# A graph network on one core: where the output bias of the last convolution is added

## The reference

```python
def _sage_conv(x, edge_index, W_l, b, W_r):
    agg = segment_sum(x[src], dst, num_segments=x.shape[0])
    mean = agg / clip(cnt, 1.0)[:, None]
    return mean @ W_l + b + x @ W_r

h = relu(_sage_conv(h, edge_index, W1_l, b1, W1_r))   # 64 -> 128
x = x + _sage_conv(h, edge_index, W2_l, b2, W2_r)     # 128 -> 64
```

## Time and profile before

| | us |
|---|---|
| median of 3 runs | 7730.98 |
| lowest and highest | 7723.53, 7738.78 |
| the profiled execution | 7742.53 |
| its span from the first to the last instruction | 7740.3 |

### The profile page before, as it was taken

How to read it: one execution, slowest core, us unless ns; L and a number is a source line. 1 busy time by engine, 2 the same in 40 slices (tenths; PEclk the granted TensorE clock), 3 DMA queues, 4 the chain that set the end, 5 groups by cost and what they waited for, 6 DMA issues and landing times.

```text
span 7740.3 us, 169629 instructions
## 1 busy us (share of the span) xinstructions
PE 6713.2 (87%) x36506; PEld 3466.6 (45%) x36667; DVE 5131.9 (66%) x16509; ACT 3383.0 (44%) x5811; POOL 4929.5 (64%) x5691
## 2 busy tenths in 40 slices
PE   6999999975777767777759999999999899998998
PEld 4777777742333333333324444444444344443443
DVE  7888888865777777777746777777777733332322
ACT  5999999943545454545423333333333301110000
POOL 4333333327777777777757777777777466663777
PEclk9999999985556666666569999999999999998999
DMA  4333333342222222222222222222222266665765
GB/s 124 96 96 97 96 97 96 96 157 67 86 81 86 81 86 82 86 82 82 86 54 61 60 62 62 61 60 60 61 61 61 52 184 171 168 166 158 199 195 159
DMA packets 773996, 769.58 MB, mean 99 GB/s; under 512 B 242490, under 2 KB 585591, under 8 KB 773815
## 3 DMA queue, kind: packets, MB, share of 16 engines
q1 hardware_dynamic: 575703, 589.32, 24.5%
q0 software_dynamic: 147776, 160.99, 10.5%
q10 hardware_dynamic: 50400, 17.87, 1.0%
HBM read 581.15 MB, written 187.29 MB: 99 GB/s over the span
## 4 chain that ended last, share of the span: by engine, by line
PE 56%; POOL 13%; issue 12%; DVE 10%; DMA 4%; DVEq 2%; ACT 2%; another core or an unknown queue 0%; ACTq 0%; POOLq 0%; SPq 0%
POOL zone L1032 10%; PE ps L2549 8%; PE ps L2388 7%; PE ps L2187 6%; PE ps L2205 5%; PE ps L2212 4%; PE ps L2554 4%; PE ps L2380 3%; DMA zone<-tab_msg,idx 3%; POOL zone L1072 3%; DVE zone L1376 2%; PE ps L2352 2%; PE ps L2203 2%; PE ps L2407 2%; PE ps L2373 1%
## 5 line engine op out<-in xcount | busy, mean ns | idle before, releaser
L1032 POOL DMA_INDIRECT zone<-tab_msg,idx x1664 | 1729.2, 1039 | 526.6 <-issue 467.8
L1032 POOL DMA_INDIRECT zone<-tab_u,idx x1664 | 1580.0, 950 | 603.7 <-issue 479.6
L2026 ACT ACTIVATE zone<-ps 128x792 fp8e4<-128x792 f32 x1200 | 963.2, 830 | 990.8 <-PE ps L2352 973.5
L1376 DVE TENSOR_TENSOR zone<-ps,zone 128x512 f32<-128x512 f32 x1664 | 1063.1, 685 | 367.7 <-PE ps L2380 233.0
L2187 PE MATMUL ps<-zone 128*128 128x64 f32 (+1 forms) x6656 | 860.0, 287 | 341.3 <-DMA zone<-tab_msg,idx 337.3
L2352 PE MATMUL ps<-zone 128*128 128x396 bf16 x2400 | 898.5, 484 | 247.8 <-ACT zone L2026 147.7
L2187 PEld LDWEIGHTS ps<-zone 128*128 128x128 f32 (+1 forms) x6656 | 758.6, 198 | 492.8 <-issue 447.0
L2388 PE MATMUL ps<-zone,w_bas 128*64 128x512 f32 x3328 | 898.7, 618 | 0.0
L2549 PE MATMUL ps<-zone 128*128 128x512 fp8e4 x3332 | 842.6, 382 | 25.4 <-DMA zone<-adj 14.8
L1661 DVE TENSOR_SCALAR zone<-tT,zone 128x392 bf16<-128x392 f16 x2400 | 777.2, 324 | 0.0
L2052 ACT ACTIVATE zone<-ps 64x512 f32<-64x512 f32 x832 | 492.4, 592 | 491.1 <-PE ps L2373 479.6
(11 more groups left out here) (324 smaller groups left out, 10390.6 us busy)
## 6 DMA issues: line engine op xcount, KB each, us to landing
zone<-adj SPq DMA_DIRECT2D x238, 768.0 KB
adj<-zone SPq DMA_DIRECT2D x150, 784.0 KB
zone<-in_dst_row SPq DMA_DIRECT2D x832, 128.0 KB, 2.7
zone<-in_ea_T SPq DMA_DIRECT2D x416, 128.0 KB, 2.5
zone<-src_lin SPq DMA_DIRECT2D x2448, 0.5 KB
zone<-adj SPq DMA_DIRECT2D x34, 896.0 KB
tab_msg<-zone SPq DMA_DIRECT2D x104, 256.0 KB, 2.1
zone<-tab_msg,idx POOLq DMA_INDIRECT x1664
```

What stands on the lines that cost most here:

```text
L1032: nc.gpsimd.indirect_dma_start(out=gat(e, u)[:, k, :], out_offset=None, in_=table, in_offset=bass.IndirectOffsetOnAxis(ap=idx[:, u, k:k + ...
L1376: nc.vector.tensor_tensor(zed[:, b % SL, :], bank(2 + b % 2), inter[:, u % 2, b % 2, :], ALU.mult) \
L2026: nc.scalar.activation(staging[m][:, :, at_ * 2 * WN:(at_ + 1) * 2 * WN].rearrange("p b (w d) -> p w b d", w=2), pair_[:, :, 0:CX].rearran ...
```

## The change

The product L2474 and its operand `b_c2` go, with the load of its right half and the clearing of its left half. ACT fetches the bias to all 128 partitions, as its first DMA of stage 0, into 64 columns of `zone` that are free there. DVE adds it to the rows of `x` of all 98 node blocks in one instruction, 128 partitions x 6272 elements, between `rest_of_sums` and `mask_far`; it first waits until the bias is there. The result is added to `x` as before.

```diff
-        b_c2 = sb("b_c2", [1, 2 * D])
+        bias_at = NB * D - D
+        assert rel_at + NGC * TL // 2 <= bias_at
+        b_out = zone[:, bias_at:bias_at + D]
...
-            (b_c2[:, D:2 * D], t["c2_b"]),
...
-        N_CONSTS = 27
+        N_CONSTS = 26
...
-                                 (w_uv[D:D + 1, 0:D], 0.0), (b_c2[:, 0:D], 0.0)):
+                                 (w_uv[D:D + 1, 0:D], 0.0)):
...
             rest_of_sums(0, RC)
+            dve.wait_ge(x_ahead, 32)
+            order(nc.vector.tensor_tensor(x[:, 0:NBS, :], x[:, 0:NBS, :], b_out.unsqueeze(1).to_broadcast([P128, NBS, D]), ALU.add))
             mask_far()
             each_turn(dve, conv_turn(0))
...
+            act.dma_start(b_out, t["c2_b"].to_broadcast([P128, D])).then_inc(x_ahead, 16)
             for slot in range(SLOTS):
                 load_own(1 if slot < 2 else SLOT2_FROM, slot)
...
-                    mm(bank(1)[:, cols], tT[:, 0, cols], w_c2[:, :], start=True, stop=False)
-                    last = mm(bank(1)[:, cols], ones[0:1, :], b_c2[:, :], start=False, stop=True)
+                    last = mm(bank(1)[:, cols], tT[:, 0, cols], w_c2[:, :], start=True, stop=True)
```

## The result

| | before | after |
|---|---|---|
| median, same chip (4 runs each) | 7732.15 | 7678.73 |
| lowest and highest | 7723.53, 7738.78 | 7672.12, 7684.55 |
| the profiled execution | 7742.53 | 7672.12 |
| its span | 7740.3 | 7670.6 |

The account below looks back on a forecast made before the run. PE's instruction stream was taken as the bound in the dense turns, a hand-over chain behind them. -37.4 - 5.8 + 6.7 + 2.4 - 0.4 = -34.5 us, median 7731.0 to 7696.5; range 7690 to 7706 (68%), with three rivals 7680 to 7711.

Parts of the forecast that it names:

- The removal in the dense turns: Stage 0's dense turns: dropping L2474 saves 0.83 us in each of 45 groups, 37.4 us.
- the neighbours could close up a little better or worse: Dense turns: products around the removed one may change spacing, 0.08 us per group either way, 3.6 us of range.
- The four groups behind: Groups after the dense turns, at low clock: the chain moves forward 1.44 us per group, 5.8 us saved.
- The stall: Before turn 1's gathered product: PE waits 7.2 us for DVE's addition; +6.7, slow clock +2.4, less other waiting -0.4 us.
- a longer addition: DVE's new instruction, estimated at 6.69 us, might take longer: +1.2 us in the range.
- The small edits: Extra bias DMA (up to 0.3 us for PE's adj wait) and one MEMSET fewer (0.14 us): taken as zero together.
- The first: Rival: PE gets past the wait for the addition or makes it up; 7687.8 us, 8%.
- The second: Rival: POOL's gathers become the bound in the dense turns; 7734 us, 5%.
- The third: Rival: the DVE addition delays POOL's gathers, another wait of up to 6.7 us; 7703 us, 6%.
- The fourth: Rival: PE's clock does not fall behind the dense turns, 8.5 us gained over four groups; 7688 us, 10%.
- The fifth: Rival: PE's clock stays low after the new wait, over three turns; 7763 us, slower, 3%.
- The remark on the wait ahead: DVE's 11.40 us wait for PE just before the addition would have hidden its cost of 6.7 us, but is unused.

Follow-up runs that it names:

- no_add: Kernel after without the addition on DVE, so the bias is left out; 7691.11 us, 0.9930 of before.
- rows128: Kernel before with the bias product over 128 stationary rows (zero-padded operand) in place of one; 7714.88 us, 0.9957 of before.
- conv1_pairs: Kernel after with conv1's four products reordered, both of 64 rows first, then both of 65; 7666.4 us, 0.9908 of before.
- both: Kernel before with its bias product kept (operand all zero) and the DVE addition put in as well; 7757.21 us, 1.0013 of before.
- add_early: Kernel after with the one addition moved ahead of rest_of_sums, before DVE's long wait; 7681.0 us, 0.9933 of before.
- the second: Kernel after, unchanged, run again on the chip of later runs; 7684.99 us beside 7733.98 for before, 0.9934.
- best: Kernel after with the addition split by group, conv1's equal-row products paired, and the bias fetched in turn 1; 7659.31 us, 0.9899 of before.
- best_wide: Kernel of best with conv1's second pair over 128 zero-padded rows in place of 65; 7652.95 us, 0.9894 of before.

## Why the prediction missed

**The removal in the dense turns: the term that was mis-sized.** "L2474 takes 0.42 + 0.41 = 0.83 us per group" was read rightly and used wrongly: it gave the whole of a gap to the product at its start. The groups of before take 1.56 us (6551.38 to 6552.94) or 1.66 us, by what they stand between, and those of after 0.44 or 0.55 us (6507.70 to 6508.25 in its timeline). Lower from lower and higher from higher, 1.12 or 1.11 us went. 45 x 1.12 = 50.4 in place of 37.4 us: 13.0 us too little. (Measured with no stall in the way, no_add, it is 50.7.) What went besides the two products, 0.22 us each, is some 0.2 us for each change of rows between them and their neighbours. The bound for this, "the neighbours could close up a little better or worse", was 0.08 us per group; it was 0.29. I took a fifth of a product for it with no row to say so, when the question "what would this product take with no such neighbour" had an answer in the trace, in L2159. One sentence had the clue in it, "that it has only one row of ones makes it no cheaper": it was not merely no cheaper, it made others dearer (rows128, conv1_pairs).

**The four groups behind.** The chain did hang on the end of L2474, as said. The same step failed for the same reason. DVE's copy started 7009.83 - 7006.83 = 3.00 us after the first L2473; in after the same copy (L1750, at 6946.36) starts 1.26 us after the first L2479 at 6945.10. So 1.74 us per group and 7.0 in all, in place of 1.44 and 5.8; the row of that stretch in the table is 7.1. The groups follow each other after 10.3 to 10.5 us, where 10.6 were forecast.

**The stall.** Right in place and size: 6.69 us as estimated from the earlier trace rows, 7.40 us of waiting for the 7.2 forecast. The clock was low for 6.1 us behind it, for the 5 forecast; by the 2.8 us of conv1_pairs behind the same stall, this length is in part chance. Together 8.4 us (both) for 6.7 + 2.4 - 0.4 = 8.7. The range also allows 1.2 us for a longer addition; no run shows that: it took 6.69 us in after and in both, with a gather of POOL beside it, and 6.68 in add_early.

**The sum mended.** -50.4 - 7.0 + 8.4 = -49.0, as measured in stage 0. With the small edits (next) it is -47.6. The medians differ by 53.4 us in the first comparison and by 49.0 in the second. A gain of 47.6 us would lie inside the range of 7680 to 7711; that the median lies 1.3 us under it is scatter. The gain that is half as large again as the forecast is not.

**The small edits.** Not nothing. The first dense product of stage 0 waits 14.6 to 14.8 us for `adj` in the three kernels that don't fetch the bias there and 16.0 to 16.2 in the seven that do, against "up to 0.3 us":

```profile
6162.08 2.45 ACTq L2080 DMA_DIRECT2D zone<-tab_h  x3
6168.85 4.83 PE L2554 MATMUL ps<-zone 128*128 128x512 fp8e4 x12 [16.01 <-DMA zone<-adj]
```

ACT's three loads behind the fetch take 2.45 us to issue, for 1.68. In best and best_wide, with the fetch in turn 1, the wait is 14.85 and 14.62 us again; they have other edits too, but in best none that runs ahead of that point. Why so small a fetch holds back the piece of `adj` was not tried.

**The rivals.** The first (the stall doesn't show) is refuted by both. The second (gathers take over): no, POOL still waits 61.2 us for PE. The third: its lock is there, the gather lasts 7.18 us beside an addition of 6.69 and 7.08 in both, and 0.94 where no instruction of DVE holds it. This is the rule of the Trainium skill, page "SBUF — State Buffer", section "SBUF: two separate sides", as the prediction told it, and the trace agrees. PE didn't feel it: it was late by the same amount. The fourth (the clock holds behind the dense turns): no, the window 6938 to 6980 has 0.50. The fifth: no, 0.99 over the turns.

**The remark on the wait ahead** ("would have hidden it") was wrong, by add_early: only 3.1 of 8.4 us.

## What to carry to other kernels

To price the removal of an instruction from a full stream, ask what its neighbours will be afterwards, and look in the same trace for products of that shape that already have such neighbours; the spacing now is only what the instruction costs with itself in between. Between small 32-bit products avoid changes of the number of stationary rows, by zero rows or by order: that alone gave 34 and 19 us here, with no work removed. Look in the trace whether a change costs before you pay for its removal, by whether the load runs ahead of its product; the one from 65 to 128 rows cost nothing. A wait of an engine is slack for a new instruction only from the point on from which nobody downstream needs what that engine does next.

## What the runs showed of the hardware

- At the full clock, 32-bit products of 128 columns start 0.22 us apart in a run of 128 stationary rows each, even where 127 of them are zero (rows128, after), and 0.42 us apart where the rows alternate (1 and 128, 64 and 65), though the one has up to 127 rows more. Each change costs 0.2 us. The weight load is 0.11 us ahead of its product inside the run and not ahead behind a change. That the late load is the cause inside PE is argued from these rows, and not shown.
- From 65 stationary rows to a dense product of 128 the load runs ahead and the product starts 0.11 us after the last record, as inside a run (after, conv1_pairs). What distinguishes this change from that of 64 to 65 stays open.
- One long DVE instruction with two 32-bit inputs in SBUF holds a gather of POOL that begins beside it: it lasts 7.18 and 7.08 us for 0.94 and ends 0.82 us after the addition of 6.69 us (after, both).
- The phases ahead of stage 0 differ by up to 31 us between kernels that are all but the same there, nearly all of it in the first two layers. The cause was not found; the spread is wider than half of the effects told of here, so these rest on the length of stage 0.
- Behind the same wait of 7.4 us the clock stayed low for 6.1 us in one profile and for 2.8 us in another (after, conv1_pairs), which is worth 1.6 us.
